# Key units one more place behind the heads, four small reorderings beside it, in a two-layer transformer kernel on one Trainium2 core

## The reference, cut to what matters

```python
x = x + mlstm(layernorm(x), ctx, ctx)          # 16 heads of 32: decay matrix D from gates, C = qk * D, C @ v
x = x + moe(layernorm(x))                      # 8 experts, 2 chosen, and a shared expert
x = x + xattn(layernorm(x), ctx)               # 16 heads of 128; k_img = rms_norm(ctx @ ki_w + ki_b), v_img = ctx @ vi_w + vi_b
x = x + ternary_linear(layernorm(x))
```

## Time and profile before

| what | value |
|---|---|
| time of the runs | 1326.87, 1315.83, 1322.72 us, median 1322.72 |
| the profiled execution's own time | 1326.44 us |
| its span, first to last instruction | 1324.7 us |
| PE busy | 1277.5 us, 96% of the span |
| DVE, ACT, POOL busy | 840.9, 739.0, 396.4 us |
| mean granted TensorE clock | 0.990 of full speed |

### The profile page before, as it was taken

One profiled execution on the slowest core, in us unless ns is written; L12 is line 12 of the kernel. 1 busy time (PEld: TensorE's weight loads), 2 busy tenths in 40 slices (PEclk: granted clock), 3 DMA queues, 4 the chain that ended last, 5 costly groups with the idle time before them and its releaser, 6 DMA issues. The chain is left out here.

```text
span 1324.7 us, 24468 instructions
## 1 busy us (share of the span) xinstructions
PE 1277.5 (96%) x7390; PEld 1061.3 (80%) x7391; DVE 840.9 (63%) x1610; ACT 739.0 (56%) x1830; POOL 396.4 (30%) x367
## 2 busy tenths in 40 slices
PE   8999999799999899999999999999999999999998
PEld 7787776577787778788877778878888898888987
DVE  2644646688788873544445477463587777777965
ACT  4325548588887441444556455454786556556561
POOL 0111003373829216599531332163010000000041
PEclk9999999899999899999999999999999999999999
DMA  7897398777875294665669776555275555555403
GB/s 226 319 378 258 128 324 292 283 243 273 294 234 191 68 362 175 217 197 165 206 203 324 236 265 190 181 193 196 114 231 164 157 164 159 157 170 153 119 28 127
DMA packets 167415, 277.06 MB, mean 209 GB/s; under 512 B 29792, under 2 KB 59232, under 8 KB 167072
## 3 DMA queue, kind: packets, MB, share of 16 engines
q1 hardware_dynamic: 141232, 219.46, 51.0%
q0 software_dynamic: 8960, 30.41, 6.7%
q10 hardware_dynamic: 17136, 26.09, 5.4%
HBM read 167.11 MB, written 108.80 MB: 208 GB/s over the span
## 5 line engine op out<-in xcount | busy, mean ns | idle before, releaser
L121 PE MATMUL banks<-of_shared_split,key_lead 128*128 128x512 f32 x256 | 105.9, 414 | 6.5 <-DVE key_trail L1453 6.5
L3048 ACT ACTIVATE prob<-banks,attend_row,rq 128x128 f32<-128x128 f32 x248 | 110.5, 470 | 0.0
L3061 ACT ACTIVATE attend_ol<-banks,of_attend_vbias 128x512 fp32r<-128x512 f32 x64 | 44.2, 691 | 116.3 <-PE banks L3260 116.3
L121 PE MATMUL banks<-wo,attend_ol 128*128 (+1 forms) x256 | 106.3, 415 | 0.0
L122 PE MATMUL banks<-of_shared_split,key_lead 128*128 128x512 f32 x256 | 101.3, 396 | 0.0
L121 PE MATMUL banks<-queries_rows_split,queries_wl 128*128 128x512 f32 x256 | 101.0, 395 | 0.2 <-DVE queries_rows_split L2683 0.2
L123 PE MATMUL banks<-of_shared_split,key_trail 128*128 128x512 f32 x256 | 101.2, 395 | 0.0
L123 PE MATMUL banks<-wo,attend_ot 128*128 (+1 forms) x256 | 100.8, 394 | 0.0
L3030 POOL TENSOR_TENSOR x_kept<-x_kept,attend_tern_bias 128x512 f32<-128x512 f32 x12 | 15.5, 1294 | 282.6 <-ACT of_attend_raw L3087 281.0
L122 PE MATMUL banks<-wo,attend_ol 128*128 (+1 forms) x256 | 100.0, 391 | 0.0
L122 PE MATMUL banks<-queries_rows_split,queries_wl 128*128 128x512 f32 x256 | 99.8, 390 | 0.0
(11 more groups left out here) (408 smaller groups left out, 3521.6 us busy)
## 6 DMA issues: line engine op xcount, KB each, us to landing
mlstm_gmax<-running_max SPq DMA_DIRECT2D x32, 512.0 KB, 6.1
k_heads<-heads_key ACTq DMA_DIRECT2D x64, 256.0 KB, 4.5
q_heads<-queries_head SPq DMA_DIRECT2D x64, 256.0 KB, 2.9
q_ahead<-q_heads SPq DMA_DIRECT2D x64, 256.0 KB, 4.2
of_attend_k<-k_heads SPq DMA_DIRECT2D x60, 256.0 KB, 4.1
of_attend_v<-v_heads SPq DMA_DIRECT2D x60, 256.0 KB, 3.2
key_raw<-in_L_xattn_ki_w SPq DMA_DIRECT2D x20, 512.0 KB, 5.0
sorted_rows<-of_shared_split SPq DMA_DIRECT2D x2, 5120.0 KB, 26.7
```

Source lines behind the costliest of these rows:

```text
L121: nc.tensor.matmul(out, lead_l, lead_r, start=first, stop=False)
L3048: ins = nc.scalar.activation(prob[:, j % 2, b, :], ps[:, j % 2, b * S:(b + 1) * S], ACT.Exp, bias=row[:, j % 2, 1, b:b + 1], scale=rq[:, b ...
L3061: nc.scalar.activation(ol[:, par, j, :], ps[:, 4 + j % 2, :], ACT.Identity, bias=vbias[:, bass.ds(quad_of(it) * 4 + j, 1)]).then_inc(ol_do ...
```

## The change

- `LAG` becomes 5, and `OPENING` has 11 entries in place of 12: one key unit fewer in the first group, later units one step later, and five in place of four behind the last head. The finishing code has one more `weight_lead`, `weight_trail`, `keep_key` and `add_square`. The first group's new tuple also sets its unit 8 at step 10, 9 at 13 and 10 at 15.
- In the first group the context sums move from steps 10 and 11 of DVE to 13 and 14, the values on POOL from 12 to 14 to 13 to 15.
- In the first group the cut for unit 3 moves from step 1 to step 0: on ACT behind `exp` and ahead of `keep_key`, on DVE behind two `decayed` and ahead of `add_square`.
- All four tail units are in the stage "heads"; the next stage's waits for the tail are gone, and its DVE work starts with `stage_rows(0)`.
- `keep_busy` at the end of "queries" issues 24 transposes in place of 14.

```diff
-TAIL_IN_HEADS = 3
+TAIL_IN_HEADS = 4
...
-    LAG = 4
-    OPENING = (-1, 0, 1, 2, 3, 5, 6, 8, 9, 11, 13, 15)
+    LAG = 5
+    OPENING = (-1, 0, 1, 2, 3, 5, 6, 8, 10, 13, 15)
...
-                    at = n - (12 if first else 5)
+                    at = n - (13 if first else 5)
...
-                    keys_at(g, n, 1, weight_lead, first)
+                    if not (first and n == 1):
+                        keys_at(g, n, 1, weight_lead, first)
                     if n + 2 < PER or g + 1 < G:
                         exp(g, n + 2, first)
+                    if first and n == 0:
+                        keys_at(g, 1, 1, weight_lead, first)
                     keys_at(g, n, -1, keep_key, first)
...
             keep_key(last, PER - LAG + 1)
+            weight_lead(last, PER - LAG + 4)
             deviation(last)
             keep_key(last, PER - LAG + 2)
             keep_key(last, PER - LAG + 3)
+            keep_key(last, PER - LAG + 4)
...
-                    if first:
+                    if first and n != 1:
                         keys_at(g, n, 1, weight_trail, first)
...
-                    at = n - (10 if first else 3)
+                    at = n - (13 if first else 3)
...
+                    if first and n == 0:
+                        keys_at(g, 1, 1, weight_trail, first)
...
             variance(last, 0)
             variance(last, 1)
             add_square(last, PER - LAG + 1)
+            weight_trail(last, PER - LAG + 4)
             factor(last)
...
             add_square(last, PER - LAG + 2)
+            add_square(last, PER - LAG + 3)
...
-            add_square(last, PER - LAG + 3)
+            add_square(last, PER - LAG + 4)
...
                 keys(G - 1, m)
-                token_sums(range(3 * (m - PER + LAG), 3 * (m - PER + LAG) + 3))
+                if m < PER - 1:
+                    token_sums(range(3 * (m - PER + LAG), 3 * (m - PER + LAG) + 3))
...
-            sp.wait_ge(tail_kept, GB - TAIL_IN_HEADS)
...
-            pool.wait_ge(tail_product, GB - TAIL_IN_HEADS)
             nc.gpsimd.memset(zeros, 0.0).then_inc(zeros_done, 1)
...
             stage_rows(0)
+            own(nc.vector.reciprocal(K.rstd[:, late], K.rstd[:, late]))
+            own(nc.vector.tensor_tensor(square[:], K.mv[:, late, 1], K.rstd[:, late], ALU.mult))
+            nc.vector.tensor_tensor(square[:], square[:], K.rstd[:, late], ALU.mult).then_inc(ms_done, 1)
+            stage_rows(1)
             dve.wait_ge(rms_done, 1)
...
-            for b in range(TAIL_IN_HEADS, GB):
-                tail_unit(nc, ps, E1.split, tail_w, b).then_inc(tail_product, 1)
             turn_rows(0, slice(0, C))
-            pe.wait_ge(tail_kept, GB - TAIL_IN_HEADS)
             turn_rows(1, slice(0, C))
...
-            keep_busy(nc, ps[:, 7, :], K.ident, 14)
+            keep_busy(nc, ps[:, 7, :], K.ident, 24)
```

More of the change, by code:

```diff
@@ L1626, in turned_and_shared @@
         across_done, upright = sem("across_done"), sem("upright")
-        tail_product, tail_kept, tail_stored = sem("tail_product"), sem("tail_kept"), sem("tail_stored")
+        tail_stored = sem("tail_stored")
         zeros = E1.split[:, 1, 1, 0].bitcast(F32)
@@ L1704, in _ @@
             first, rest = slice(0, 1), slice(1, C)
-            for b in range(TAIL_IN_HEADS, GB):
-                act.wait_ge(tail_product, b - TAIL_IN_HEADS + 1)
-                nc.scalar.activation(tail_v[:, :, b, :], ps[:, TAIL_BANKS[b], :].rearrange("p (h e) -> p h e", h=4), ACT.Copy
-                                     ).then_inc(tail_kept, 1)
             turned_rows(0, slice(0, C))
@@ L1724, in _ @@
             late = slice(EARLY, B)
-            own(nc.vector.reciprocal(K.rstd[:, late], K.rstd[:, late]))
-            own(nc.vector.tensor_tensor(square[:], K.mv[:, late, 1], K.rstd[:, late], ALU.mult))
-            nc.vector.tensor_tensor(square[:], square[:], K.rstd[:, late], ALU.mult).then_inc(ms_done, 1)
             def stage_rows(g):
@@ L1740, in _ @@
             own(nc.vector.tensor_tensor(E1.scale[:, late], K.rstd[:, late], square[:], ALU.mult))
-            stage_rows(1)
             nc.vector.tensor_tensor(fold[:], K.ident[0:2 * E, 0:E], K.ident[0:2 * E, E:2 * E], ALU.add).then_inc(fold_done, 1)
```

## The result

The changed kernel is slower by half a per cent: median 1328.33 us of 16 runs (1323.08 to 1334.06), against 1323.25 for the kernel before (16 runs); the ratio, estimated over all runs, is 1.0049 [1.0037, 1.0062] (the medians lie 5.1 us apart). On another chip the unaltered changed kernel gave 1.0059 [1.0043, 1.0076]. The prediction was 1318.7 us with a range from 1309 to 1326.

A forecast was written before the change was run, and what follows sets the result against it. With PE busy for 96% of the span, only its idle stretches and low-clock matmuls could give time. Terms of 4.2 + 0.3 - 0.5 + 0 = 4.0 us gained, off a median of 1322.72, gave 1318.7 us, range 1309 to 1326.

The forecast's parts named there:

- Groups two to four: Later groups of "heads": same matmuls, order shifted one step; +0.3 us gained, bounds -2 and +3.
- Cost zero: Groups two to four: SP's maxima requests come 2.8 us later, covered by 9.3 us before the exponent, so nothing lost.
- the sum: Whole kernel: 4.2 + 0.3 - 0.5 + 0 = 4.0 us gained, so 1318.7 us.
- The slower rival: Groups two to four: 18 tight cuts fall behind DVE's work, each costing 1.1 us; net 11.8 slower, 1334; chance 0.09.
- the mild form: Groups two to four: the rival of tight cuts with 8 us lost, giving 1327 us.
- First group: First group of "heads": earlier unit 3 cut, later context sums and one unit fewer gain 4.2 us; bounds 2.3 and 7.7.
- The term of 1.6 us for the cut of unit 3: First group: the earlier cut lets all that follows come 1.6 us sooner, bounds 0 and 3.5.
- The end of "heads": Before the barrier: PE stops 2.6 us for unit 63's late trail cut, bounds 0.5 and 4.7; barrier opens at 453.0.
- tail and barrier: End of "heads" and start of the next stage together: 0.5 us lost, bounds +1.6 and -2.6.
- PE's clock behind the barrier: Behind the barrier: by the skill's rule the clock would rise later with only transposes there; no row showed whether so.
- The rival of b_tail: Behind the barrier: transposes alone keep the clock low, losing the tail unit's saving; ratio 1.000 to 1.001, no chance given.
- The transposes ahead of "attend": End of "queries": ten more transposes last 1.2 us, perhaps repaid by the clock; net 0, bounds -0.6 and +0.9.

The follow-up runs named there:

- a_sp: The changed kernel with SP's wait for the end of a group's units at step 11 in place of 9: 1321.09 us, 0.9996 of the kernel before.
- b_ctx: The kernel before with only the first group's context sums at steps 13 and 14 and the values one step later: 1317.75 us, ratio 0.9964.
- b_tail: The kernel before with only the four tail units in the stage and the new order behind the barrier: 1320.73 us, ratio 0.9985.
- b_busy: The kernel before with only 24 transposes in place of 14 at the end of "queries": 1323.61 us, ratio 1.0004.
- a_sp63: a_sp with the trail cut of unit 63 between the two halves of the variance: 1318.27 us, 0.9960 of the kernel before.
- b_sp8: The kernel before with only SP's wait and the eight split loads two steps earlier, at step 8: 1334.20 us, ratio 1.0084.

## Why the prediction was wrong, step by step

**Groups two to four: this step failed.** It saw the right event, "the maxima behind it are asked for one unit (2.8 us) later against the heads", and the right price without cover, "2.8 per group". Then it looked at one reader of the mask, the exponent 9.3 us behind the earlier trace rows, and wrote zero. The mask has another reader of its time: what is queued behind it on POOL. The additions to x were next, DVE's row statistics wait for them, and the gather that PE needs stands behind the statistics. The kernel before already showed DVE waiting 3.9 us for x once, in a row that the prediction did not read. The step that failed is therefore the "Cost zero" for SP's later request. Measured: +4.5 and +8.0 us of stretch in two profiles, 8.3 us by a_sp, against the +0.3 (up to 3) of the sum. The request was in fact 4.9 us later, not 2.8, since the eight loads and a raw weight ahead of it took longer too. Of the four groups, only the second and third have this wait.

**The slower rival named the wrong mechanism.** It put the danger on tight trail cuts. They did rise, from 3.2 to 4.5 us in the middle stretch, and stayed at 4.6 in a_sp, which is level with before. Its time of 1327 for the mild form is near the result by accident.

**First group: right in sum, by another way.** The prediction had 4.2 us at equal work; 7.7 - 2.8 = 4.9 between the two profiles, and the sums alone (b_ctx) gave about 5 in the runs. But the first stretch of unchanged code scatters, from 50.2 us (b_tail) to 53.5 (b_busy), and before's profile is at the long end, so the whole gain against a usual run is less: against 50.2 it is 50.2 - 45.6 - 2.8 = 1.8. The expected remainder of DVE's wait, 4 us, was none: the sums followed a decay without idle time. Nor was there PE's stop of about 5 us ahead of the scores; the longest stop of the group is 2.21 us at 230.64, for a trail cut.

```profile
231.11 0.68 DVE L1167 SCALAR_TENSOR_TENSOR heads_cmat<-banks,heads_dec 128x512 f32<-128x512 f32 x1
231.70 1.26 DVE L1184 TENSOR_REDUCE heads_cmean<-mlstm_ctx 128x16 f32<-128x512 f32 x2
232.89 0.68 DVE L1167 SCALAR_TENSOR_TENSOR heads_cmat<-banks,heads_dec 128x512 f32<-128x512 f32 x1
```

The scores started at 235.01, 45.6 behind the start, where 238.4 - 193.6 = 44.8 was predicted. The term of 1.6 us for the cut of unit 3 is not there. PE's stop for that cut went from 1.95 to 0.76 us, but a later cut then made PE stand:

```profile
207.56 0.50 PE L121 MATMUL banks<-of_shared_split,key_lead 128*128 128x512 f32 x1 [2.00 <-DVE key_trail L1463]
```

The group's fourth set of scores came 35.4 us behind its first, in place of 34.3. In the six profiles with the early cut it is 33.8 to 37.1 us, in the eight without it 33.5 to 34.3. It was not tried alone. All that the group gained lies between its fourth set of scores and the next group's first, where the context sums and the unit that left had been.

**The end of "heads": sized right within its bounds.** PE stopped for unit 63, as said, for 1.57 us (1.28 in the repeat), where 2.6 stood in the sum and 0.5 to 4.7 in the bounds:

```profile
430.79 0.50 PE L121 MATMUL banks<-of_shared_split,key_lead 128*128 128x512 f32 x1 [1.57 <-DVE key_trail L1463]
```

DVE stood twice for ACT at the end. The first root came behind the copy of a tail unit. The second waited for PE's sums, so PE's work did set the end of the stage, as had been forecast:

```profile
444.41 0.23 DVE L1330 RECIPROCAL heads_msq<-heads_msq 128x12 f32<-128x12 f32 x1 [2.25 <-ACT heads_msq L1147]
...
447.09 0.27 ACT L1150 ACTIVATE rk<-banks,eps 128x16 f32<-128x16 f32 x1 [0.19 <-PE banks L1404]
...
447.40 0.25 DVE L1337 RECIPROCAL rk<-rk 128x16 f32<-128x16 f32 x1 [2.14 <-ACT rk L1150]
```

Behind the barrier the third `stage_rows` ended at 456.25 + 1.91 = 458.16, 10.0 us behind the 448.20 at which DVE started; 9.3 had been worked out. From the fourth group's last scores to that end it is 61.4 us in place of 57.6, so with 2.8 for the unit that came, tail and barrier lost 1.0 us, where the sum had 0.5. That tail and barrier are a small gain without the late cut is what b_tail (0.9985) shows; what the late cut takes from it is the 1.3 to 1.6 us of the stop at the least, and 3.3 us by the last stretches of a_sp and a_sp63; the sum had 2.6.

**PE's clock behind the barrier.** With no other matmuls there, the 32 transposes took 5.98 us:

```profile
450.83 5.98 PE L1836 MATMUL banks<-ident,of_x_normal 128*128 128x128 f32 x32 [3.78 <-DVE of_x_normal L1733]
```

Before, behind 12 matmuls, they took 4.10. They now start the stretch, so more of them run at the 1.2 GHz level. DVE's chain hides the 1.9 us, as it bounds this place. The view of the stretches shows when the clock rose, in the changed kernel:

```profile
455.25:455.50 0.25, 0.25 (x3) 0.25 (x2) 0.25 (x1) 0.13 (x1) 0.00 (x0) 0.50 0.71 16
...
455.75:456.00 0.25, 0.25 (x5) 0.25 (x3) 0.25 (x1) 0.25 (x2) 0.00 (x0) 1.00 0.98 41
```

and in the kernel before:

```profile
456.00:456.25 0.25, 0.25 (x3) 0.25 (x2) 0.00 (x0) 0.25 (x1) 0.25 (x2) 0.50 0.00 0
...
456.50:456.75 0.25, 0.25 (x4) 0.25 (x3) 0.00 (x0) 0.21 (x1) 0.25 (x2) 1.00 0.00 0
```

PE had been idle for 3.78 us and then did nothing but transposes from 450.83 on, and the clock rose to the 2.4 GHz level none the less, and no later than behind the 12 matmuls that started at 450.20. "TensorE: Matmul & The Clock Gate", Part 4, of the Trainium skill says that transposes do not count as work for the clock as matmuls do; for these float32 transposes the rows disagree. The rival of b_tail, that transposes alone would keep the clock low and lose the gain again, did not come true either (0.9985).

**The transposes ahead of "attend": right in the sum.** The row is now 24 transposes of 2.78 us and an idle 0.60 in place of 1.42:

```profile
953.31 2.78 PE L129 MATMUL banks<-ident 128*128 128x128 f32 x24
956.68 1.02 PE L3288 MATMUL banks<-ones,queries_total 128*128 128x1 f32 x8 [0.60 <-PEq L87]
957.92 1.16 PE L3241 MATMUL banks<-attend_kn,q_ahead 128*128 128x128 f32 x8 [0.22 <-DVE attend_kn L3117]
```

Before, the same first scores took longer:

```profile
961.09 1.71 PE L3241 MATMUL banks<-attend_kn,q_ahead 128*128 128x128 f32 x8 [0.22 <-DVE attend_kn L3117]
```

There the granted clock fell from 1.00 to 0.50 at about 961.5 and was back at 965; in b_busy it stayed at 1.00 from the transposes to 965.92. But it is not always so: the first scores took 1.16 us in six of the seven profiles with 24 transposes (1.55 in a_sp) and in two of the seven with 14 (b_ctx, b_ctx_tail), 1.54 to 1.97 in the other five. More often at the full clock is what the rows show, and it is far below what the medians can tell: 1.0004. Whether it is the count of transposes or the shorter idle time behind them is not separated.

**The sum.** It was made against the profiled execution of before, 3.2 us slower than that kernel's median, and the same 4.0 us were taken from the median. With SP mended (a_sp) the change is worth 0.5 us with an interval from -0.9 to 2.1, not 4.0; with the stop for unit 63 removed (a_sp63) some 5. So the prediction's total, though not each of its parts, fits a kernel that is two positions in the order away from the one it was asked about.

## What to carry to other kernels

Where an engine's instruction is made later, slack must be counted for every instruction queued behind it on its engine, and for what these release, not only for the reader of its own result. A wait in a queue of transfers has a window, bounded by the requests behind it that are due and by its own loads' reader; when a stream of work is shifted against another, each such wait has to be placed anew. And before a few microseconds are read from two profiles, cut them at common work and look at how much unchanged stretches differ.

## What the runs showed beside it

- Code that is the same in all kernels, ahead of the heads, ended between 188.7 and 193.6 us in the 14 profiles. A single profiled execution can hide or invent 4 us.
- The first transposes behind the barrier are a common point for PE, not for DVE. In the nine profiles with all four tail units in the stage the time from there to the end of the span is 870.5 to 873.7 us, in the five with three of them 867.9 to 870.7. What PE gains ahead of that point is partly given back behind it.
- A stop of PE of a few microseconds can cost more than itself: in b_sp8, with stops for the gather of 4.3 and 5.0 us, the middle stretch has a granted clock of 0.96 in place of 1.00, and the same 1276 matmuls are busy 158.0 us in place of 153.3. In the changed kernel, with stops of 2.0 and 2.1, the clock stayed at 1.00.

```profile
241.31:411.07 169.76, 158.03 (x1276) 125.52 (x1276) 122.81 (x185) 134.63 (x303) 80.88 (x84) 0.96 0.70 242
```
